# The repeated rows of a unit in one 128-partition transfer, not three, from a longer list of rows in DRAM

## The reference

```python
xk = x0                                   # (2048, 32, 16)
for W in (W0, W1, W2):                    # (32, 32, 64), (32, 64, 64), (32, 64, 64)
    xk = relu(einsum('bmd,bhd,mhk->bkd', x0, xk, W))
    outs.append(sum(xk, axis=2))
h = concatenate([concatenate(outs, axis=1), dense_ctx], axis=1)
h = maximum(h @ W_top1 + b_top1, 0)
h = maximum(h @ W_top2 + b_top2, 0)
y = h @ W_top3                            # (2048, 1)
```

## Time and profile before

| | us |
|---|---|
| median of three runs | 1255.26 |
| lowest and highest run | 1247.16, 1269.19 |
| the profiled execution | 1254.39 |
| its span, from first to last instruction | 1252.6 |
| PE busy | 1204.9 (96%) |
| DVE busy | 1150.4 (92%) |
| POOL busy | 682.9 (55%) |
| ACT busy | 522.6 (42%) |

### The profile page before, as it was taken

One profiled execution on the slowest core, in us unless ns is written; L12 is line 12 of the kernel. 1 busy time (PEld: TensorE's weight loads), 2 busy tenths in 40 slices (PEclk: granted clock), 3 DMA queues, 4 the chain that ended last, 5 costly groups with the idle time before them and its releaser, 6 DMA issues.

```text
span 1252.6 us, 16643 instructions
## 1 busy us (share of the span) xinstructions
PE 1204.9 (96%) x6396; PEld 606.0 (48%) x6396; DVE 1150.4 (92%) x534; ACT 522.6 (42%) x786; POOL 682.9 (55%) x705
## 2 busy tenths in 40 slices
PE   0899999999999999999999999999999999999997
PEld 0443444444444555455555555555555555555344
DVE  3389999999999999999999999999999999999894
ACT  0444444444344444344444444444443444444321
POOL 6757676857667573745647375564737551210201
PEclk9999999999999999999999999999999999999999
DMA  5399999999999999999999889999999999987650
GB/s 121 78 226 223 250 250 241 236 229 227 237 240 245 233 234 227 231 246 244 245 242 242 233 233 242 236 232 240 240 234 244 241 240 242 239 239 234 195 149 1
DMA packets 73685, 277.50 MB, mean 222 GB/s; under 512 B 29819, under 2 KB 38805, under 8 KB 41318
## 3 DMA queue, kind: packets, MB, share of 16 engines
q1 hardware_dynamic: 54388, 267.09, 85.9%
q0 software_dynamic: 16384, 4.23, 3.1%
q10 hardware_dynamic: 2834, 5.12, 1.6%
HBM read 272.15 MB, written 4.20 MB: 221 GB/s over the span
## 4 chain that ended last, share of the span: by engine, by line
PE 72%; DMA 12%; DVE 6%; POOL 5%; issue 4%; SPq 1%; ACT 0%; DVEq 0%; ACTq 0%
PE accs L788 54%; DMA kept<-x_rows 11%; PE acc L742 9%; DVE prod L662 6%; POOL emb L308 5%; PE wide L711 3%; PE xe L799 2%; PE xe L808 2%; PE wide L694 1%; SPq L271 1%; DMA emb<-in_tbl,idx 1%; PE wide L718 0%; PE xe L818 0%; DMA idx<-in_ids 0%; PE accs L784 0%
## 5 line engine op out<-in xcount | busy, mean ns | idle before, releaser
L788 PE MATMUL accs<-prod,w2s 128*64 128x512 f32 x2016 | 935.8, 594 | 3.4 <-DVE prod L662 2.9
L788 PE MATMUL accs<-prod,w1s 128*64 128x512 f32 x2016 | 929.0, 593 | 0.0
L662 DVE TENSOR_TENSOR prod<-kept,xe 128x2048 f32<-128x2048 f32 x256 | 583.7, 2281 | 33.9 <-PE accs L788 27.3
L662 DVE TENSOR_TENSOR prod<-kept,xp 128x2048 f32<-128x2048 f32 x256 | 583.4, 2281 | 17.4 <-ACT xp L481 7.2
L308 POOL DMA_INDIRECT emb<-in_tbl,idx x512 | 484.7, 947 | 208.2 <-issue 119.1
L788 PEld LDWEIGHTS accs<-prod,w1s 128*64 128x64 f32 x2016 | 271.4, 137 | 288.4 <-issue 186.4
L788 PEld LDWEIGHTS accs<-prod,w2s 128*64 128x64 f32 x2016 | 267.5, 137 | 106.1 <-issue 68.5
L742 PE MATMUL acc<-sq,u 128*64 128x512 f32 x640 | 218.9, 593 | 0.3 <-ACT sq L437 0.3
L467 ACT ACTIVATE sq<-wide 128x1024 f32<-128x1024 f32 (+1 forms) x155 | 145.5, 939 | 169.2 <-PE wide L711 81.1
L347 POOL TENSOR_TENSOR x3f<-x3f 64x512 f32<-64x512 f32 x31 | 39.6, 1279 | 132.7 <-ACT x3f L517 132.3
L742 PEld LDWEIGHTS acc<-sq,u 128*64 128x64 f32 x640 | 82.3, 137 | 59.8 <-issue 27.9
(11 more groups left out here) (85 smaller groups left out, 512.1 us busy)
## 6 DMA issues: line engine op xcount, KB each, us to landing
kept<-x_rows SPq DMA_DIRECT2D x252, 512.0 KB, 6.1
kept<-x_rows SPq DMA_DIRECT2D x504, 256.0 KB, 8.2
emb<-in_tbl,idx POOLq DMA_INDIRECT x512, 2.6
x_rows<-x3f ACTq DMA_DIRECT2D x31, 128.0 KB, 8.2
prod<-in_w_all ACTq DMA_DIRECT2D x1, 512.0 KB, 6.1
w1s<-in_L_rec_W SPq DMA_DIRECT2D x4, 128.0 KB, 3.3
w2s<-in_L_rec_W SPq DMA_DIRECT2D x4, 128.0 KB, 3.4
wt<-in_W_top SPq DMA_DIRECT2D x1, 512.0 KB
```

The lines of the kernel that those rows point to most:

```text
L662: nc.vector.tensor_tensor(prod[layer][:, q % BUFS[layer], :, :], kept[:, q % KEPT, :, :], xp[layer][:, :].unsqueeze(1).to_broadcast([128, ...
L788: last = mm(accs[64 * (layer - 1):64 * layer, s % 2, :], wk[layer][:, t, :], prod[layer][:, q % BUFS[layer], i, :], start=t == 0, stop=t = ...
```

## The change

Each half of 64 partitions had one set of 16 fields. Now each group of 8 partitions has its own: group e (partitions 8e to 8e + 7) holds in step t the field (t + 2e) % 32. A row h is in groups h // 8 and h // 8 + 8, whose starts differ by 16, so that every pair of row and field still comes once. The weights are laid out on the host in the same manner, as two whole 128-partition arrays, and come in one load each.

So that each group reads four rows one after the other, the list of a block in DRAM goes on past row 31 with rows 0 to 13 again (`LISTED` is 46): a second store, of 14 rows, follows the first, on SP for pair 0 and on ACT for the others, and `s_stored` counts 32 for a pair. A unit is then one transfer: 16 starts 2 rows apart, each read by 8 partitions, 8 KB to a partition. DVE waits for 16 on `s_kept`. The selectors of the first four units follow the turning: 16 small copies, which DVE now makes after `u`, and PE waits for them only ahead of the first made row.

```diff
-PARTS = [(1, 32, 96), (0, 0, 32), (0, 96, 128)]
+CHUNKS, CHUNK = 16, 8
+TURN_BY = 2
+AGAIN = M // 2 + TURN_BY * (CHUNKS - 1) - M
+LISTED = M + AGAIN
...
-                for lo, r in ((0, 0), (32, 1), (64, 1), (96, 0)):
-                    sp.dma_start(wk[l][lo:lo + 32, :, :],
-                                 w.rearrange("(r t) h k -> r h t k", r=2)[r, lo % 64:lo % 64 + 32])\
-                        .then_inc(s_w12, 16)
+                sp.dma_start(wk[l][:, :, :], w).then_inc(s_w12, 16)
...
-                for r, lo, hi in PARTS:
-                    row = 16 * r + GT * g
-                    sp.dma_start(
-                        kept[lo:hi, n % KEPT, :, :].rearrange("p a n -> p (a n)"),
-                        x0_rows[s // 2, s % 2:s % 2 + 1, row:row + GT, :].rearrange("j m n -> j (m n)")
-                        .to_broadcast([hi - lo, GT * BLK])).then_inc(s_kept[n % KEPT], 16)
+                first = ((s // 2 * 2 + s % 2) * LISTED + GT * g) * BLK
+                sp.dma_start(
+                    kept[:, n % KEPT, :, :].rearrange("p a n -> p (a n)"),
+                    bass.AP(x0_rows.tensor, first, [[TURN_BY * BLK, CHUNKS], [0, CHUNK], [1, GT * BLK]]))\
+                    .then_inc(s_kept[n % KEPT], 16)
...
-            sp.dma_start(x0_rows[0].rearrange("j m n -> m j n"), fields[0]).then_inc(s_stored[0], 16)
+            sp.dma_start(x0_rows[0, :, 0:M, :].rearrange("j m n -> m j n"), fields[0]).then_inc(s_stored[0], 16)
+            sp.dma_start(x0_rows[0, :, M:LISTED, :].rearrange("j m n -> m j n"), fields[0][0:AGAIN])\
+                .then_inc(s_stored[0], 16)
...
-                    act.dma_start(x0_rows[p].rearrange("j m n -> m j n"), fields[p % 2])\
+                    act.dma_start(x0_rows[p, :, 0:M, :].rearrange("j m n -> m j n"), fields[p % 2])\
+                        .then_inc(s_stored[p % 2], 16)
+                    act.dma_start(x0_rows[p, :, M:LISTED, :].rearrange("j m n -> m j n"), fields[p % 2][0:AGAIN])\
                         .then_inc(s_stored[p % 2], 16)
...
-            for c in range(2):
-                field = sums[:, ST - 1, M + 16 * c:M + 16 * c + 2 * rows].rearrange("p (a b) -> p b a", a=2)
-                nc.vector.tensor_copy(pick[:, :, 64 * c:64 * c + 64].rearrange("p b (a q) -> p b a q", a=2),
-                                      field.unsqueeze(3).to_broadcast([128, rows, 2, 32])).then_inc(s_pick, 1)
...
+            for e in range(CHUNKS):
+                nc.vector.tensor_copy(pick[:, :, CHUNK * e:CHUNK * e + CHUNK],
+                                      sums[:, ST - 1, M + TURN_BY * e:M + TURN_BY * e + rows].unsqueeze(2)
+                                      .to_broadcast([128, rows, CHUNK])).then_inc(s_pick, 1)
...
-                        dve.wait_ge(s_kept[q % KEPT], 48 * loads)
+                        dve.wait_ge(s_kept[q % KEPT], 16 * loads)
...
-            pe.wait_ge(s_pick, 2)
...
+            pe.wait_ge(s_pick, CHUNKS)
...
-            pe.wait_ge(s_w12, 16 * 8)
+            pe.wait_ge(s_w12, 16 * 2)
...
+    e, t, h = _np.arange(128)[:, None] // CHUNK, _np.arange(M // 2)[None, :], _np.arange(128)[:, None] % K
+    w1, w2 = (dram(f"{n}_laid", _np.asarray(inputs[f"L0_rec_{n}"])[(t + TURN_BY * e) % M, h]) for n in ("W1", "W2"))
+    x0_rows = nc.dram_tensor("x0_rows", (PAIRS, 2, LISTED, BLK), FP32, kind="Internal").ap()
```

More of the change, by code:

```diff
@@ L290, in _ @@
                     p = n // 8
-                    sp.wait_ge(s_stored[p % 2], 16 * (p // 2 + 1))
+                    sp.wait_ge(s_stored[p % 2], 32 * (p // 2 + 1))
                 keep_rows(n)
@@ L463, in square @@
                     if p >= 2:
-                        act.wait_ge(s_stored[p % 2], 16 * (p // 2))
+                        act.wait_ge(s_stored[p % 2], 32 * (p // 2))
                     nc.scalar.copy(fields[p % 2], wide[0:M, :, :]).then_inc(s_fields, 1)
@@ L923, in dram @@
         return nc.dram_tensor(f"in_{name}", a.shape, _mybir.dt.from_np(a.dtype), kind="ExternalInput").ap()
-    args = {n: dram(n, inputs[n]) for n in inputs if n not in ("dense_ctx", "L0_rec_W0")}
+    args = {n: dram(n, inputs[n]) for n in inputs if n not in ("dense_ctx", "L0_rec_W0", "L0_rec_W1", "L0_rec_W2")}
     p = _np.arange(128)[:, None, None]
@@ L946 @@
     dense_t = _np.concatenate([_np.asarray(inputs["dense_ctx"]).T, _np.ones((1, B), _np.float32)])
-    x0_rows = nc.dram_tensor("x0_rows", (PAIRS, 2, M, BLK), FP32, kind="Internal").ap()
+    e, t, h = _np.arange(128)[:, None] // CHUNK, _np.arange(M // 2)[None, :], _np.arange(128)[:, None] % K
+    w1, w2 = (dram(f"{n}_laid", _np.asarray(inputs[f"L0_rec_{n}"])[(t + TURN_BY * e) % M, h]) for n in ("W1", "W2"))
+    x0_rows = nc.dram_tensor("x0_rows", (PAIRS, 2, LISTED, BLK), FP32, kind="Internal").ap()
     out = nc.dram_tensor("out_0", (B, 1), FP32, kind="ExternalOutput").ap()
@@ L950 @@
           args["W_top1"], args["b_top1"], args["W_top2"], args["b_top2"], args["W_top3"],
-          dram("w0_pairs", w0_pairs), dram("w0_all", w0_all), args["L0_rec_W1"], args["L0_rec_W2"],
+          dram("w0_pairs", w0_pairs), dram("w0_all", w0_all), w1, w2,
           dram("sel_sums", sel_sums),
```

## The result

The changed kernel takes **1270.74 us** (median of 4 runs, 1268.85 to 1271.99); the kernel before, on the same chip, 1253.8 us (4 runs). The ratio is 1.0139 with a 95% interval of 1.0093 to 1.0186: slower by 1.4%, where the forecast was 0.4% faster. The time lies in the range, between the forecast's 1249 and the first rival's 1303. The profiled span is 1270.0 us, 17.4 more than before.

A forecast was written before the change was run, and what follows sets the result against it. PE's pace was taken to bound the kernel, with slow kept-row transfers losing 5.6 us in early rounds; all other terms were 0, so 1254.4 - 5.6 = 1249 us, with an overall range of 1241 to 1335.

The forecast's parts named there:

- the first rival: Kept-row transfers: one transfer runs at the slow rate all the time, 231 GB/s, +49 us, 1303 us; chance 0.39.
- PE's floor: Eight-unit rounds: 36.41 us each at PE's own pace; 11 early rounds took 406.12 against 400.5, so 5.6 us lost.
- The step that failed: Rate of the new 128-partition transfer: taken as 373 GB/s, 2.9 us a unit, under PE's 4.55, so the 5.6 us go.
- The lower bound of 204: Rate of the new transfer at its slow end, as the 32-partition transfers: 204 GB/s, 5.38 us a unit.
- SP's issues: SP issues 252 times, not 756, at some 0.6 us each; SP waits for DVE anyway: 0 us.
- The second store: 31 extra stores on ACT's queue, 9.6 us in all, where ACT waits for PE: 0 us, at worst +9.6.
- The later start of the kept rows: Pair 0's second store on SP starts kept transfers about 0.3 us later, still ahead of DVE's product at 68.00: 0 us.
- The selectors: 16 small copies on DVE behind u, 3.5 to 10.4 us, hidden in DVE's idle time: 0 us; uncovered 2.2 to 9.1.
- Weight loads: Eight loads become two; SP issues nothing for units before 53.44 and the weights are needed after that: 0 us.
- Hidden anyway: Rival: the transfers were hidden already, so faster ones change nothing; 1254 to 1255 us, chance 0.10.
- Fewer engines: Rival: a source with 16 outer steps uses fewer than 16 DMA engines; with half, +153 us, 1407 us; chance 0.03.
- What would show it: Right: in 250:330 DMA share well under 0.86, rounds of 36.4 us; first rival: share 1 or more, DVE waiting every unit.

The follow-up runs named there:

- 32 starts: Changed kernel with fields turned for each 4 partitions, 32 starts of 4 partitions in one transfer: 1248.89 us, run again 1250.66 us.
- one row: Changed kernel with the unit's transfer reading one start row for all 128 partitions, written as 128 outer steps of 0: 1247.46 us, ratio 0.9936.
- the halves: Kernel before with its parts recut into two 64-partition transfers, partitions 0 to 63 and 64 to 127, one store: 1271.65 us, ratio 1.0115.
- 44 copies: Changed kernel with each unit's 128 starting rows copied into lists in DRAM, 128 steps on both sides, 44 selector copies: 1253.77 us, ratio 0.9991.
- 128 steps: Changed kernel with 128 outer source steps: all reading one start row, 1247.46 us (0.9936), or 128 different starts, 1247.59 us (0.9938).
- small ranges of 8 starts: Partitions 0 to 31 and 96 to 127 in the changed kernel with fields turned per 4 partitions and three transfers a unit: 1309.7 us, ratio 1.0396.

## Why the prediction was wrong

The reading of the kernel before held in the main: slow transfers cost it a few us, and the versions that run at 400 GB/s without lists take 1247 to 1251 us, where the sum said 1249. The size was off. PE's floor of 36.41 us a round was taken from the later rounds; the first 11 need 398.30 us with 32 starts and 398.27 with one row, 36.21 each, so 7.8 us were lost there and not 5.6. That 32 starts come out at the forecast's 1249 is in part luck, since they lose 3.05 us at the start. So is it that the changed kernel lies within 2% of the kernel before, to which the prediction gave 0.60: it got there with the slow transfers, not without them.

**The step that failed** is the rate: "The row nearest by its destination is the load of in_w_pairs, 128 partitions, with 373 GB/s in 2.70:3.40. I take 373". It measured 210 to 238 at the start, with the transfers of the first units. The nearest row was chosen by its destination, and the destination does not decide alone: with the same 128 partitions, 57:62 has 411 GB/s with 128 outer steps in the source and 228 with 16. These 16, each for eight partitions, were the one thing that was new. The row is also loose as a rate of one load: in_w_all and others were under way in that stretch, and the same stretch of the kernel after has 305 GB/s. The lower bound of 204 was the nearer one.

**The first rival** had the rate: the whole megabyte goes as slowly as the slow half did (210 to 238 GB/s at the start; that half had 204 and 220). Its size was off. It held 231 GB/s for all of the 246 units, 4.75 us each, 49 us in all, added to 1254.4, which holds today's loss already (on the floor's 1249 it would be 1298); measured were 4.82 us a unit from 151 to 267, but then the rate climbs (256 and 262 in two slices near the middle of the span) until PE sets the pace again, at 36.28 us a round (611.23 to 647.51). The whole span grew by 17.4 us, 1.3 of them at the start. No run shows why 231 should hold, and not 220 or 204: the changed kernel has 231 in 250:330 and 239 on the mean from the 11th to the 37th slice.

What the outer steps do is shown as far as this: with 128 partitions on the other side, 16 outer steps give 228 GB/s, 32 give 402, 128 give 411, and the DMA share is 1.00 to 1.01 in each. The runs do not show why; which engine wrote which partitions, and how the pieces of a transfer spread, no run here shows. What the partitions do is shown by the halves' 212 against 423.

**Point by point.** *SP's issues*, 0 us: right, SP only waits longer. *The second store*, 0 us: right, ratio 0.9998 by itself; on ACT's queue it is one issue of 0.44 us. A store does stand on the changed kernel's chain once (106.25, 11.99 us), but the halves, with a single store, have the same at 105.66 (11.55 us): what is late there is the slow queue. *The later start of the kept rows*, 0 us: right as to cause; the 1.3 us at the start come from gathers. *The selectors*, 3.5 to 10.4 us and hidden: they took 2.23 us, below both bounds, but were not free. The term looked at DVE's own queue alone. The gather that met the 16 copies took 2.02 us in place of 0.94, with 32 copies 3.73 and with 44 copies 4.58, and PE's first matmul waits for gathers. With one row the copies were stretched instead (2.60 us), and PE began at 35.59. So they cost about 1.1 us here and 2.8 with 32 starts; the lines show that gather and copies coincide, and no run tests it alone. *Weight loads*, 0 us: nothing speaks against it. *Hidden anyway*: fell, since faster transfers gave the rounds back, and with 128 steps the whole kernel is faster (0.9936 and 0.9938, both intervals below 1). *Fewer engines*: fell for the whole transfer, since the share of the 16 engines is 1.02 in 57:62; for the small ranges of 8 starts, with a share of 0.77, it stays open. *What would show it*: a share of 1 or more, long rounds and DVE waiting, as the text said for the first rival; only that DVE would wait in every unit was too much (51 waits for 246 units).

## What to carry to other kernels

Here a transfer's rate went with the outer steps of its source (228 GB/s with 16, 402 with 32, 411 with 128) and with the partitions that it covers (212 against 423), not with its bytes alone: where 128 partitions are written, try a broadcast with 32 or 128 outer steps in the source, and time the very form before a plan rests on it. Where a queue runs close to its need (231 of 241 GB/s), a forecast for a slower transfer should ask what the queue and its buffers absorb; here one buffer less, 9 for 10, cost some 38 us (1308.54 against 1270.74). Work moved to an idle place of its own engine can still delay another engine (the gather beside the 16 copies took 2.02 us, its neighbours 0.94): look at what runs beside it. A transfer count that falls is no gain by itself when the issuing engine was waiting anyway (SP waited 629.0 us for DVE with 756 transfers and 880.7 with 252).

## What was not expected of the hardware

The same 8 KB read for all partitions moves at 411 GB/s when it is written as 128 steps and at 228 when it is written as 16 times 8 (both in 57:62), with the same 42430 packets. A transfer of 64 partitions from partition 32 has 423 GB/s; with two of them, from 0 and from 64, the queue has 212. And in one and the same form the rate of a full queue is no constant: 210 GB/s at 62:68, 231 at 250:330 and up to 268 in a slice of the changed kernel, and 229 instead of 239 on the mean with one buffer less.
